# Two block tables instead of one in a routed expert layer: the first 15 blocks come from the first 22 tiles, and expert numbers are loaded one register at a time

## What is computed

```python
x = x + attn(layernorm(x))          # 16 heads of 8; running sums of k*v and k, y = q.kv / q.ksum, projection
h0 = layernorm(x)
logits = h0 @ Wr + br               # [.., 8]
route_w = softmax(logits); take the top 2; renormalise over these two
h = relu(h0 @ W1[e] + b1[e])        # 128 -> 512
expert_out = h @ W2[e] + b2[e]      # 512 -> 128
x = x + sum over the two experts of routed[e] * expert_out[e]
```

## Time and profile before

| | us |
|---|---|
| median of three runs | 420.39 (420.29 to 422.45) |
| profiled execution | 424.1 |
| its span | 421.8 |
| busy PE / DVE / POOL / ACT | 313.9 / 294.8 / 268.6 / 192.7 |

### The profile page before, as it was taken

The page is one execution under the profiler, slowest core; times in us unless marked ns, Lnnn a source line. Parts: engine busy times, 40 slices in busy tenths (PEclk is TensorE's granted clock), DMA queues, the critical chain, the costliest instruction groups (busy, mean ns, idle before and its releaser), DMA issues.

```text
span 421.8 us, 8197 instructions
## 1 busy us (share of the span) xinstructions
PE 313.9 (74%) x2452; PEld 241.2 (57%) x2452; DVE 294.8 (70%) x691; ACT 192.7 (46%) x479; POOL 268.6 (64%) x249
## 2 busy tenths in 40 slices
PE   0799696987899869889743204999989988999400
PEld 0688464664676646657432103887878877788300
DVE  4979748669699898798981650675765665656367
ACT  2588205475512411431313002776767765767263
POOL 4479335899647887887767770366656755757600
PEclk9999887898999998998955555999999999999955
DMA  7980000000000110000111113132222222311188
GB/s 215 322 223 2 2 0 1 1 0 2 0 2 13 33 33 13 32 28 26 44 46 38 51 58 101 51 91 71 85 78 77 79 77 67 87 54 39 50 336 262
DMA packets 24064, 29.39 MB, mean 70 GB/s; under 512 B 3820, under 2 KB 18676, under 8 KB 24023
## 3 DMA queue, kind: packets, MB, share of 16 engines
q1 hardware_dynamic: 18582, 18.99, 15.0%
q0 software_dynamic: 4544, 9.38, 6.8%
q10 hardware_dynamic: 896, 0.50, 0.5%
HBM read 16.19 MB, written 12.67 MB: 68 GB/s over the span
## 4 chain that ended last, share of the span: by engine, by line
PE 38%; DVE 25%; issue 12%; POOL 11%; ACT 7%; DMA 5%; SPq 1%; POOLq 0%; DVEq 0%; ACTq 0%
POOL y_rows L500 7%; PE ps L1088 7%; DVE work L825 5%; DVE nd L831 4%; POOL x_rows L455 3%; PE ps L1259 3%; PE ps L1240 3%; PE ps L1242 3%; PE ps L1241 3%; PE ps L1260 3%; PE ps L1264 3%; PE ps L1087 2%; DVE y_s L842 2%; ACT xs L590 2%; PE ps L1061 2%
## 5 line engine op out<-in xcount | busy, mean ns | idle before, releaser
L500 POOL DMA_INDIRECT y_rows<-wraw,yid x78 | 87.4, 1121 | 60.1 <-ACT wraw L665 47.6
L425 POOL TENSOR_TENSOR kvt<-qk,v 128x1024 f32<-128x1024 f32 x32 | 67.5, 2136 | 30.9 <-PE ps L1092 20.1
L1088 PE MATMUL ps<-kvt,tri 128*128 128x384 f32 (+1 forms) x192 | 73.8, 498 | 11.5 <-DVE work L825 11.5
L455 POOL DMA_INDIRECT x_rows<-rows,pos_i x64 | 62.6, 979 | 25.2 <-issue 17.3
L657 ACT ACTIVATE wraw<-ps,b1s 128x256 f32<-128x256 f32 x156 | 61.4, 490 | 7.3 <-PE ps L1242 4.8
L998 DVE CAST wraw<-wraw 128x1024 f16<-128x1024 f32 x39 | 27.1, 694 | 49.1 <-ACT wraw L657 49.0
L1088 PEld LDWEIGHTS ps<-kvt,tri 128*128 128x128 f32 x192 | 38.9, 210 | 33.7 <-issue 18.8
L825 DVE TENSOR_TENSOR work<-ps,qk 128x1152 f32<-128x1152 f32 x32 | 42.2, 1350 | 12.1 <-PE ps L1092 11.8
L1240 PE MATMUL ps<-wraw,w1h 128*128 128x256 f16 x156 | 43.5, 279 | 8.6 <-ACT wraw L642 4.9
L1002 DVE TENSOR_TENSOR wraw<-wraw 128x1024 f16<-128x1024 f32 x39 | 47.8, 1225 | 1.3
L1241 PE MATMUL ps<-wraw,w1h 128*128 128x256 f16 x156 | 43.4, 278 | 0.0
(11 more groups left out here) (205 smaller groups left out, 643.1 us busy)
## 6 DMA issues: line engine op xcount, KB each, us to landing
wraw<-x_rows SPq DMA_DIRECT2D x39, 130.0 KB, 2.2
qk<-y_rows SPq DMA_DIRECT2D x8, 512.0 KB, 6.7
wraw<-in_L_ffn_W_dram SPq DMA_DIRECT2D x1, 2048.0 KB, 12.6
out_dram<-x SPq DMA_DIRECT2D x8, 256.0 KB, 4.5
x<-in_L_attn_x_dram SPq DMA_DIRECT2D x3, 512.0 KB, 9.6
y_rows<-wraw,yid POOLq DMA_INDIRECT x78, 2.7
x_rows<-empty SPq DMA_DIRECT2D x9, 130.0 KB, 4.1
x_rows<-rows,pos_i POOLq DMA_INDIRECT x64, 2.3
```

What stands on the lines that cost most here:

```text
L425: nc.gpsimd.tensor_tensor(kvt[:, u % RING, a].rearrange("p (j h i) -> p j h i", j=DH, i=DH), k.unsqueeze(1).broadcast_to([P, DH, H, DH]), ...
L455: nc.gpsimd.indirect_dma_start(out=x_rows, out_offset=bass.IndirectOffsetOnAxis(ap=pos_i[:, c, t:t + 1], axis=0), in_=rows[:, t, :], in_of ...
L500: nc.gpsimd.indirect_dma_start(out=y_rows, in_=ysb[:, n % XG, g], in_offset=None, out_offset=bass.IndirectOffsetOnAxis(ap=yid[:, n, g:g + ...
L1088: nc.tensor.matmul(o, tri[:, :], kv[a][:, cols], start=(a == 0), stop=True)
```

## The change

There are now two tables. The first is made from the counts of groups 0 to 3 and holds only whole blocks: `N1 = (2 * 22 * 128 - 8 * 255 + 255) // 256 = 15`, which exist however the rows are spread. (The change's own note speaks of 14; the formula and the built program have 15.) The second holds the other 24 blocks, made from all counts less what the first used. SP's loads of blocks 0 to 14 wait for the first table and for the first 44 scatters, those of block 15 on for the second table and all scatters. What remains of the routing of groups 4 to 6 is moved: on DVE the first table stands before `split_low(5)`, and `positions(6)` and the second table stand in pieces behind blocks 0 to 10; on PE `ranks(4)` stands behind `turn_group(5)`, `ranks(5)` and `ranks(6)` among the first blocks; on POOL three scatters stand before `layer_norm_2(6)`, and the last 12 go two by two ahead of the y scatters of blocks 0 to 5. The operations of `block_table` are the bodies of `table_full` to `table_diag`, which are called for both tables (the first of them rounds a count down for the first table and up for the second). Blocks of the first table need no `aside`, so their `y_rows_of` is one operation. The y buffer has eight places, not six, and lies in `kvt`. PE and ACT load one register per block. The gates and their exponential move behind the blocks.

```diff
+    FIRST = 4
+    T1 = TPU * sum(GROUPS[:FIRST])
+    N1 = (TOP * T1 * P - E * (SLOTS - 1) + SLOTS - 1) // SLOTS
+    N2 = NBLK - N1
+    SPREAD = 8
+    YG = 8
-            sp.wait_ge(table_done, 2)
-            for c in range(TOP):
-                sp.wait_ge(x_scattered[c], 16 * NT)
             for n in range(NBLK):
                 b = n % XG
+                if n in (0, N1):
+                    i = 0 if n == 0 else 1
+                    sp.wait_ge(table_done, 2 * (i + 1))
+                    for c in range(TOP):
+                        sp.wait_ge(x_scattered[i][c], 16 * (NT - T1 if i else T1))
...
             layer_norm_2(NG - 2)
-            first = SCATTERS - TOP * TPU * sum(GROUPS[-3:])
-            for n in range(sent, first):
+            for n in range(sent, sent + 3):
                 scatter_x(n)
             layer_norm_2(NG - 1)
-            for n in range(first, SCATTERS):
+            early = TOP * (T1 + TPU * GROUPS[FIRST])
+            for n in range(sent + 3, early):
                 scatter_x(n)
             for n in range(NBLK):
+                for m in range(early + 2 * n, min(early + 2 * n + 2, SCATTERS)):
+                    scatter_x(m)
                 scatter_y(n)
...
-                if n % PER == 0:
-                    act.load(regs, table_i[0:1, 1, n:n + PER])
+                if n == N1:
+                    act.wait_ge(table_done, 4)
+                act.load(regs[n % 2:n % 2 + 1], table_i[0:1, 1, n:n + 1])
...
+            def counts(i):
+                dve.wait_ge(cnt_done, i + 1)
+                nc.vector.tensor_copy(cnt8[:, 1], ps[:, 5 + i, (0, T)[i]:(0, T)[i] + E]).then_inc(cnt_out, 1)
+                dve.wait_ge(cnt_out, i + 1)
...
+            def table_expert(i):
+                if i == 0:
+                    link(nc.vector.tensor_scalar(used[:, 0], ends, float(N1), None, ALU.min))
+                    link(nc.vector.tensor_scalar(used[:, 1], cnt8[:, 0], float(N1), None, ALU.min))
+                    link(nc.vector.tensor_tensor(used[:, 2], used[:, 0], used[:, 1], ALU.subtract))
+                else:
+                    link(nc.vector.tensor_tensor(cnt8[:, 0], cnt8[:, 0], used[:, 2], ALU.subtract))
...
-            choose(NG - 3)
             statistics(U - 1)
             moments_2(NG - 1)
-            positions(NG - 3)
-            for g in (NG - 2, NG - 1):
-                split_low(g)
-                choose(g)
-                positions(g)
-            block_table()
+            choose(FIRST)
+            positions(FIRST)
+            counts(0)
+            table_full(0)
...
+            table_diag(0)
+            table_copies(0)
+            split_low(NG - 2)
+            choose(NG - 2)
+            positions(NG - 2)
+            split_low(NG - 1)
+            choose(NG - 1)
...
                 if n + 2 < NBLK:
                     y_rows_of(n + 2)
+                if n == 0:
+                    positions(NG - 1)
+                    counts(1)
+                    table_full(1)
+                if n == 1:
+                    table_ends(1)
...
+                if n == 6:
+                    table_bounds(1)
+                    table_diag(1)
+                if n == SPREAD + 1:
+                    dve.wait_ge(y_out, SPREAD + 1)
+                    table_copies(1)
+                if n == SPREAD + 2:
+                    foreign_slots()
+            gates()
...
-            ranks(NG - 3)
-            for g in (NG - 2, NG - 1):
-                pe.wait_ge(rank_out, g)
-                turn_group(g)
-                logits(g)
-                ranks(g)
+            def spread(i):
+                n = (N1, N2)[i]
+                pe.wait_ge(diag_done, 5 * (i + 1))
+                nc.tensor.matmul(ps[:, 5 + i, (0, T)[i]:(0, T)[i] + 5 * n].rearrange("p (k n) -> p k n", k=5),
+                                 ones[:, :], diag[:, :, 0:n], start=True, stop=True).then_inc(spread_done, 1)
+            pe.wait_ge(m_done, TPU * U)
+            counts(0)
+            turn_group(NG - 2)
+            ranks(FIRST)
+            logits(NG - 2)
+            pe.wait_ge(cnt_out, 1)
+            spread(0)
+            turn_group(NG - 1)
+            logits(NG - 1)
...
             def up(n):
-                if n % PER == 0:
-                    load_experts(n)
-                e = pe.snap(experts[n], min_val=0, max_val=E - 1)
+                if n == N1:
+                    pe.wait_ge(table_done, 4)
+                pe.load(regs[n % 4:n % 4 + 1], table_i[0:1, 1, n:n + 1])
+                e = pe.snap(regs[n % 4], min_val=0, max_val=E - 1)
...
             def down(n):
...
+                if n == 0:
+                    pe.wait_ge(cnt_out, 2)
+                if n == 1:
+                    pe.wait_ge(rank_out, NG)
+                if n == SPREAD - 1:
+                    pe.wait_ge(y_out, n)
+                if n == SPREAD:
+                    pe.wait_ge(y_out, n)
+                    spread(1)
...
             turn_block(0)
             turn_block(1)
+            ranks(NG - 2)
             up(0)
             turn_block(2)
             up(1)
             turn_block(3)
+            ranks(NG - 1)
+            counts(1)
```

More of the change, by code:

```diff
@@ L56, in block_kernel @@
     in_group = [g for g in range(NG) for _ in range(GROUPS[g])]
+    FIRST = 4
+    T1 = TPU * sum(GROUPS[:FIRST])
+    N1 = (TOP * T1 * P - E * (SLOTS - 1) + SLOTS - 1) // SLOTS
+    N2 = NBLK - N1
+    assert N1 >= 10 and FIRST == NG - 3
+    SPREAD = 8
+    part_of = [0 if t < T1 else 1 for t in range(NT)]
     SCATTERS = 2 * NT
@@ L259, in block_kernel @@
         pos_done = sem("pos_done")
-        x_scattered = [sem(f"x_scattered{c}") for c in range(TOP)]
+        x_scattered = [[sem(f"x_scattered{i}_{c}") for c in range(TOP)] for i in range(2)]
         cnt_done = sem("cnt_done")
+        cnt_out = sem("cnt_out")
         diag_done = sem("diag_done")
@@ L274, in block_kernel @@
         y_out = sem("y_out")
-        y_scattered = [sem(f"y_scattered{b}") for b in range(XG)]
+        y_scattered = [sem(f"y_scattered{b}") for b in range(YG)]
         y_in = [sem(f"y_in{g}") for g in range(Y_LOADS)]
@@ L340, in _ @@
                              ).then_inc(loaded[b], 16)
-            for b in range(XG):
-                sp.wait_ge(y_scattered[b], 16 * GPB * len(range(b, NBLK, XG)))
+            for b in range(YG):
+                sp.wait_ge(y_scattered[b], 16 * GPB * len(range(b, NBLK, YG)))
             for g in range(Y_LOADS):
@@ L943, in block_table, with table_full, table_ends @@
+            full, ends, sums, mine = t8[:, 0, 0], t8[:, 1, 0], cnt8, t8[:, 2]
+            def table_full(i):
+                link(nc.vector.tensor_scalar(cnt_i[:, :], cnt8[:, 1], float(SLOTS - 1) if i else 0.0, None, ALU.add))
                 link(nc.vector.tensor_scalar(cnt_i[:, :], cnt_i[:, :], SLOTS.bit_length() - 1, None, ALU.logical_shift_right))
                 link(nc.vector.tensor_copy(full, cnt_i[:, :]))
+            def table_ends(i):
+                if i == 1:
+                    link(nc.vector.tensor_tensor(full, full, used[:, 2], ALU.subtract))
@@ L964, in block_table @@
                 link(nc.vector.tensor_tensor(t1[:, 11:12], t1[:, 3:4], t1[:, 6:7], ALU.subtract))
-                count["chain"] += 1
-                dve.wait_ge(chain, count["chain"])
-                for i in range(5):
-                    nc.vector.tensor_scalar(diag[:, i, :], ident[:, 0:NBLK], t1[:, 7 + i:8 + i], None, ALU.mult).then_inc(diag_done, 1)
-                dve.wait_ge(spread_done, 1)
-                spread = ps[:, 6, 0:5 * NBLK].rearrange("p (i n) -> p i n", i=5)
-                nc.vector.tensor_copy(table_i[:, :, :], spread[:, 0:2, :]).then_inc(table_done, 1)
@@ L972, in block_table, with table_diag @@
-                nc.vector.tensor_copy(table_f[:, :, :], spread[:, 2:5, :]).then_inc(table_done, 1)
-                dve.wait_ge(table_done, 2)
-                over_n = slot_f[:, :].unsqueeze(1).broadcast_to([P, NBLK, GPB])
-                over_g = lambda i: table_f[:, i, :].unsqueeze(2).broadcast_to([P, NBLK, GPB])
+            def table_diag(i):
+                n = (N1, N2)[i]
+                for k in range(5):
+                    nc.vector.tensor_scalar(diag[:, k, 0:n], ident[:, 0:n], t1[:, 7 + k:8 + k], None, ALU.mult).then_inc(diag_done, 1)
@@ new lines, in table_copies @@
+            def table_copies(i):
+                n, n0 = (N1, N2)[i], (0, N1)[i]
+                dve.wait_ge(spread_done, i + 1)
+                spread = ps[:, 5 + i, (0, T)[i]:(0, T)[i] + 5 * n].rearrange("p (k n) -> p k n", k=5)
+                nc.vector.tensor_copy(table_i[:, :, n0:n0 + n], spread[:, 0:2, :]).then_inc(table_done, 1)
+                nc.vector.tensor_copy(table_f[:, :, n0:n0 + n], spread[:, 2:5, :]).then_inc(table_done, 1)
+                dve.wait_ge(table_done, 2 * (i + 1))
@@ L1139, in logits @@
                 pe.wait_ge(x2_done, min(G_LAST[g] + 3, U))
-                if ranked_by(G_LAST[g] + 3):
```

(20 more changed lines are left out.)

129 lines of the change are left out of this document (76 added, 53 removed).

## The result

The changed kernel takes 408.7 us (median of four runs, 406.79 to 409.99); the kernel before, beside it on the same chip, 421.4 (median of four). The ratio is 0.968, 95% interval 0.961 to 0.975. The forecast was 396.0, with 393 to 406 as its range: the sign is right, the gain of 12.7 us is about half of the 24.4 that were forecast, and the time lies above the range.

A forecast was written before the change was run, and what follows sets the result against it. TensorE bounds the expert blocks, and POOL's x scatters keep them from beginning; -18.0 + 1.2 + 0.3 - 8.6 + 0.7 = -24.4, subtracted from the median of 420.39, gives 396.0 us, range 393 to 406.

The forecast's parts named there:

- Term 1: Start of the expert blocks: the first table lets `up(0)` begin at 241.7 instead of 259.67, -18.0 us.
- Term 2: First blocks: remaining routing on DVE and TensorE delays `down(0)` and the cast of block 1, +1.2 us.
- the second spread: Second table's spread on TensorE among the blocks: +0.3 us.
- Term 3: TensorE's and ScalarE's register loads, one per block: hidden, so the gaps of eight-register loads go, -8.6 us.
- Rivals 2 and 4: TensorE's loads: partly in the open, 406, chance 0.09; or each empties its queue, time 430, chance 0.04.
- The second table's gate: SP's load of block 15, waiting for the last x scatter and second table: costs nothing, 3 us to spare.
- POOL as the next limit: POOL's x and y scatters at 1.38 us each: POOL just catches up with TensorE by block 36, +0.7 us.
- Rival 1: POOL stays behind to the end, or late x scatters make block 15 wait: 400 to 413, chance 0.12.
- The 1.60: POOL's cost per scatter in a pair paced by TensorE (3.19 for two): POOL late by 16 us.
- rival 3: TensorE's clock: two more blocks at 0.50, at most 3.19 us each, make 402, chance 0.08.

The follow-up runs named there:

- the first experiment: The changed kernel with all twelve last x scatters ahead of the first y scatter on POOL: 402.3 us, ratio 0.954 to the kernel before.
- all three edits: The changed kernel with last x scatters ahead of the first y, subtraction in two instructions, `ranks(4)` ahead of `turn_group(5)`: 393.6 us, ratio 0.931.

## Why the prediction missed, point by point

**Term 1, the early start: right.** The first block load was due near 237 and goes at 235.8; `up(0)` was due at 241.7 and starts at 240.72 (-19.0 for -18.0). Counted from the 44th scatter of x it is -18.2 (36.55 us before, 18.37 now).

**Term 2, the first blocks: right.** `up(0)` to `down(0)` is 7.38 us (7.65 forecast), `down(1)` 3.63 later. The 28 table operations behind blocks 1 to 10 cost TensorE nothing that shows; the second spread, in the distance to `down(8)`, cost 0.22 (0.3).

**Term 3, the loads: right.** They take 0.302 us each on TensorE, as the rows of its loads tell (answering: shortest, median, longest in ns):

```profile
L1332 PEldq TENSOR_LOAD <-table_i x39: 297/302/482, 240.0 to 362.9; - x39
```

and are hidden: between blocks 1 and 35 `down` has two distances over 3.3 us, ahead of blocks 8 and 12, and neither comes from a load. Rivals 2 and 4 are out. The page DMA: Bandwidth & Descriptors of the Trainium skill (Latency and other measured facts) has a floor of about 0.6 us for a `tensor_load`; these 39 contradict it by half.

**The second table's gate: wrong by 1.8 us.** It had 3 us to spare in my working. The last x scatter starts at 281.66 and not near 277, SP's next load goes at 284.59, and TensorE waits ahead of block 12's `down`, which comes 4.99 us after the one before it:

```profile
286.85 0.40 PE L1324 MATMUL ps<-ident_h,wraw 128*128 128x128 f16 x4 [1.19 <-DMA wraw<-x_rows]
```

The x scatters lie between y scatters, and one of each two is held like them (1.61 to 1.67 us). With all of them in front, as in the first experiment, the gap is gone. It isn't in the result, as POOL sets the end.

**POOL as the next limit: the step that failed.** The term stood in the sum as +0.7, a choice between nothing and the 2.2 us at 1.43 per scatter; it measured 10.1, the last y 15.9 us behind the last `down` and not 5.8. The term said that a y or x scatter under way costs 1.38 us with its issue, "as only some meet DVE", so that POOL reaches block 36 at 365.1. It reaches it at 378.60. Of the 13.5 us, 3.7 come by block 6 (22 scatters from 250.96 to 286.04, 1.59 each, less a first y 0.9 us early), and 9.8 over the 30 pairs after it, 3.09 each and not 2.76 (3.19 from block 20 to 30; the last few, which meet no DVE work, 2.52). Had each scatter cost 1.38, the sum would have held, as the halved subtraction shows (1.40 each over the first 22 scatters, 1.37 over the next 25 pairs, and 397.0 us).

The 1.38 came from rows in which the pair starts when y arrives. Those rows show POOL waiting for TensorE. The term needed the opposite case, a POOL that never waits, and there a scatter starts early in the subtraction or ahead of the cast and gets another price. In the earlier trace rows the 1.30 and 1.38 already were scatters held by the subtraction, only shortly, as it had 0.5 us to go; I read them as the cost of the first of a pair. Rival 1 had the outcome, POOL behind to the end, with the right range (400 to 413), and I gave it 0.12; it did not have the holder, and no row stood behind its 1.5 per scatter. The 1.60 stood in the term as an outer case. What spoke against the rival was that x scatters beside other DVE work had kept 1.26. That reading looked at how busy DVE was and not at what it ran. The trace before has both cases, POOL's and DVE's timelines:

```profile
145.90 0.96 POOL L455 DMA_INDIRECT x_rows<-rows,pos_i  x1 [0.31 <-issue]
144.42 2.60 DVE L825 TENSOR_TENSOR work<-ps,qk 128x1152 f32<-128x1152 f32 x2
226.87 1.28 POOL L455 DMA_INDIRECT x_rows<-rows,pos_i  x1 [0.53 <-issue]
226.82 0.43 DVE L860 TENSOR_TENSOR rows<-xs,rows 128x256 f16<-128x256 f32 x1 [6.03 <-ACT rows L594]
```

The scatter at 145.90 starts early in the second of two products of 1.3 us each, which read one input from PSUM (`ps`), and takes 0.96; of the 14 x scatters that start in such a product with more than 0.2 us of it to run, 12 do (the other two 1.06 and 1.22). The one at 226.87 starts in a subtraction of only 0.43 us with both inputs in SBUF and takes 1.28. So the price was there to be read: not how long DVE's instruction is decides, but which one it is. That the place of the inputs is the reason fits these rows; no run varied it by itself.

The Trainium skill (SBUF — State Buffer, Who interferes with whom), applied to the cast, gave 3.21 us per pair and a lateness of 16 us in the prediction's working. The pair is 3.19, but that the two lie so near is luck: 3.21 adds the cast's 0.69 to 2.52, while 3.19 is TensorE's block, to which the subtraction locks the pair, and it stays with the cast in halves. The same section of the Trainium skill says that a DVE instruction with two inputs in SBUF contends with a GpSimd instruction that reads SBUF; the runs with the subtraction in halves and without it agree, if the scatter's reading is what is held, which no run shows. The Trainium skill's section also tells of a probe in which `tensor_tensor` did not stall a DMA, and infers as the reason that making descriptors needs the port pair's write interface, which `tensor_tensor` leaves free. This scatter is stalled: 1.62 us beside the whole subtraction, 0.96 without it.

**The clock (rival 3): not seen.** It rises from 0.50 to 1.00 near 246 us, ahead of `down(0)`, and stays there until TensorE has no more blocks; the mean from 264 to 390 is 0.94 as that window holds its idle end.

## What to carry to other kernels

The cost of an instruction on an engine that waits is not its cost when it stops waiting: before taking a price for a queue that will run back to back, look at what stands beside it at the new phase, not at the mean of the old one. Where a long periodic instruction of one engine holds another engine's, both periods can lock, and a lag is then not worked off; cutting the long instruction in two freed it here at no cost that shows (ratio 1.001 in the kernel before). Two parts of a change that uncover the same next limit don't add up, so price that limit first.

## What was not expected of the hardware

A POOL scatter that starts within DVE's 1.23 us subtraction (128x1024, both inputs in SBUF) ends 0.83 or 0.84 us after it, in all 33 cases of the changed kernel with more than 0.13 us of the subtraction to run. As a free scatter takes 0.96, one that starts in the last 0.13 us loses nothing, and so does one that starts ahead of the subtraction. Halves let scatters through: in that run one starts at 332.87 with 0.20 us of the second half to run and takes 1.03, and one at 300.23 with 0.19 of the first half to run takes 1.02, though the second half has begun by its end. A cast holds a scatter likewise where it began first (0.09 us ahead of the one at 296.37 in the changed kernel: 1.43), and one that begins 0.44 us into a scatter makes it 1.25. So in the earlier trace rows the scatter began first and was yet the one that waited.

Two of the chips ran the blocks at 3.57 and 3.61 us (medians) instead of 3.19; the kernel before takes 434.9 and 437.8 there. In the changed kernel's trace from one of them TensorE has gaps of 0.25 to 1.15 us in mid-block from 258 to 277 us, whose cause the trace gives as issue. Two `down` lie 13.4 us apart there, near 265 and 278, and the granted clock falls to 0.50 from 270 to 282. From 300 to 380 the clock is 1.00, there is one such gap (0.17), TensorE counts as busy for 78.28 of the 80 us, and yet blocks are long: ScalarE's copy of y begins 1.35 us after the row of `down`'s last matmul ends (313.71 and 315.06), on the other chip 0.04 (322.59 and 322.63), so TensorE is done later than its rows, whose ends are modelled, say. Why these chips do that stays open. The kernel with all three edits has not been run on one.
